# Cross-attention scores and weighted sums per head, in tiles of TensorE's array

## What is computed

```python
def _L0_xattn_ref(query, key, value, Wq, Wk, Wv, Wo, bo):
    DIM = 512
    NUM_HEADS = 16
    ...
    q = (query @ Wq).reshape(B, L, H, D).transpose(0, 2, 1, 3)
    k = (key @ Wk).reshape(B, S, H, D).transpose(0, 2, 1, 3)
    v = (value @ Wv).reshape(B, S, H, D).transpose(0, 2, 1, 3)
    attn = jnp.einsum('bhld,bhsd->bhls', q * SCALE, k)
    attn = jax.nn.softmax(attn, axis=-1)
    x = jnp.einsum('bhls,bhsd->bhld', attn, v)
    x = x.transpose(0, 2, 1, 3).reshape(B, L, C)
    return x @ Wo + bo
...
x = x + _L0_xattn_ref(_layernorm(x, axis=-1), ctx_1024, ctx_1024, ...)
x = x + _L0_attn_ref(_layernorm(x, axis=-1), ...)
x = x + _L0_ffn_ref(_layernorm(x, axis=-1), ...)
```

## Time and profile before

| what | value |
|---|---|
| median of three runs | 2842.11 us (2841.47 to 2845.34) |
| the profiled execution | 2842.77 us |
| its span in the trace | 2841.0 us |
| PE busy | 2720.9 us (96%), 17864 matmuls |
| DVE, ACT, POOL busy | 1657.8, 1246.9, 774.1 us |
| cross attention, by its first key matmul and the last adds of outputs | 142.89 to about 1933 us |

### The profile page before, as it was taken

One profiled execution on the slowest core, in us unless ns is written; L12 is line 12 of the kernel. 1 busy time (PEld: TensorE's weight loads), 2 busy tenths in 40 slices (PEclk: granted clock), 3 DMA queues, 4 the chain that ended last, 5 costly groups with the idle time before them and its releaser, 6 DMA issues. The chain is left out here.

```text
span 2841.0 us, 53482 instructions
## 1 busy us (share of the span) xinstructions
PE 2720.9 (96%) x17864; PEld 1635.0 (58%) x17864; DVE 1657.8 (58%) x3658; ACT 1246.9 (44%) x2898; POOL 774.1 (27%) x1530
## 2 busy tenths in 40 slices
PE   7999999999999999999999999995898998998999
PEld 4555555555555555555555555553466666666666
DVE  7645555555555555555555555556666666676675
ACT  4344444444444444444444444442444444444444
POOL 2133333333333333333333333321111111111110
PEclk9999999999999999999999999997899999999999
DMA  3311111111111111111111111103100000000000
GB/s 137 108 44 63 43 42 42 42 42 42 42 43 48 42 42 42 42 42 42 42 44 47 42 42 42 42 13 100 52 31 16 16 30 15 15 30 15 15 23 16
DMA packets 65959, 118.47 MB, mean 42 GB/s; under 512 B 12017, under 2 KB 32497, under 8 KB 65393
## 3 DMA queue, kind: packets, MB, share of 16 engines
q1 hardware_dynamic: 65904, 117.76, 12.7%
HBM read 109.06 MB, written 8.65 MB: 41 GB/s over the span
## 5 line engine op out<-in xcount | busy, mean ns | idle before, releaser
L746 DVE SCALAR_TENSOR_TENSOR kT_lo<-psum,kT_hi 128x512 f16<-128x512 f32 x256 | 177.0, 692 | 447.3 <-ACT kT_hi L677 447.3
L681 ACT ACTIVATE v_hi<-psum 128x512 f16<-128x512 f32 x256 | 153.1, 598 | 551.1 <-PE psum L836 551.1
L123 POOL TENSOR_TENSOR c_lo<-ctx_raw,c_hi 128x1024 f16<-128x1024 f32 x128 | 272.3, 2128 | 447.7 <-ACT c_hi L673 422.4
L836 PE MATMUL psum<-c_hi,xWk_hi 128*128 128x512 f16 x1024 | 388.1, 379 | 0.5 <-PEq L143 0.5
L836 PE MATMUL psum<-xWv_hi,c_hi 128*128 128x512 f16 x1024 | 388.1, 379 | 0.0
L836 PE MATMUL psum<-xWv_lo,c_hi 128*128 128x512 f16 x1024 | 388.1, 379 | 0.0
L836 PE MATMUL psum<-xWv_hi,c_lo 128*128 128x512 f16 x1024 | 388.1, 379 | 0.0
L836 PE MATMUL psum<-c_lo,xWk_hi 128*128 128x512 f16 x1024 | 388.1, 379 | 0.0
L836 PE MATMUL psum<-c_hi,xWk_lo 128*128 128x512 f16 x1024 | 388.1, 379 | 0.0
L752 DVE SCALAR_TENSOR_TENSOR v_lo<-psum,v_hi 128x512 f16<-128x512 f32 x256 | 177.1, 692 | 360.7 <-ACT v_hi L681 360.7
L687 ACT ACTIVATE e<-psum,neg_max 128x257 f32<-128x257 f32 x512 | 237.3, 476 | 281.7 <-DVE neg_max L741 281.7
(11 more groups left out here) (227 smaller groups left out, 5715.6 us busy)
## 6 DMA issues: line engine op xcount, KB each, us to landing
ctx_raw<-in_ctx_main SPq DMA_DIRECT2D x128, 512.0 KB, 3.3
xs<-in_x SPq DMA_DIRECT2D x8, 1024.0 KB, 5.4
v_rep<-v_last_rows SPq DMA_DIRECT2D x512, 16.0 KB, 2.3
xb<-in_x SPq DMA_DIRECT2D x16, 512.0 KB, 3.6
out<-res_out SPq DMA_DIRECT2D x32, 256.0 KB, 2.1
ffn_raw<-in_w_t SPq DMA_DIRECT2D x11, 512.0 KB, 3.8
res<-in_w_t SPq DMA_DIRECT2D x5, 512.0 KB, 4.0
xs<-in_late_w SPq DMA_DIRECT2D x2, 1024.0 KB, 4.8
```

The source lines that it names most:

```text
L123: nc.gpsimd.tensor_tensor(c_lo[u // 2][:, :, u % 2, :], c_raw[u % 2][:, :, :], c_hi[u // 2][:, :, u % 2, :], ALU.subtract).then_inc(c_lo_d ...
L681: nc.scalar.mul(v_hi[u][:, t, :], v_bank(t), W_UNSCALE).then_inc(v_hi_done, 1)
L746: nc.vector.scalar_tensor_tensor(out=kT_lo[r][:, m, :, 0:S], in0=k_bank(m), scalar=W_UNSCALE, in1=kT_hi[r][:, m, :, 0:S], op0=ALU.mult, op ...
L836: mm = nc.tensor.matmul(bank, a, b, start=(n == 0), stop=(n == len(steps) - 1))
```

## The change

Scores and outputs are made per head, on parts of PE's array. A matmul whose operands lie in a strip of 32 partitions, and whose result goes to a strip of 32 PSUM partitions, takes one 32 x 32 tile of the array; one with 128 operand partitions and 32 result partitions takes a column strip of 128 x 32.

- `score`: weights are the queries of one head, 32 x 32, taken from `q_hi` or `q_lo`, two buffers each; the head (g, h) sits in partition strip h and writes to partition strip g of bank h. There are 3 passes x 4 x 4 = 48 matmuls of 257 columns, the passes outermost. No zeros are multiplied.
- `outputs`: for each h, six steps of four matmuls, one for each strip g: weights are 128 context tokens by the 32 latent rows of a head, 32 columns of values are streamed. There are 4 x 6 x 4 = 96 matmuls into bank 3, partition strip g, columns 32 h to 32 h + 31.
- The roles of g and h are swapped in PSUM and behind it: `gather_output` is one 128 x 128 add where there were four of 32 x 128; the value rows of the last token are kept in natural order; Wo's rows are permuted on loading, by four DMAs (`load_output_weight`) instead of one.
- POOL: `stage_queries` makes two copies of 128 x 128 where `spread` made eight of 32 x 128, and may run one element further ahead, since there are two buffers; the two memsets go.
- PE's five waits before the scores are put before the last matmul of the `values` ahead of them (`score_may_start`).

```diff
-                nc.scalar.mul(vl[:, :].rearrange("p (h g d) -> p g h d", h=4, g=KC),
-                              v_last_bank.rearrange("p (g h d) -> p g h d", h=4, g=KC),
-                              W_UNSCALE).then_inc(vl_done, 1)
+                nc.scalar.mul(vl[:, :], v_last_bank, W_UNSCALE).then_inc(vl_done, 1)
...
-        bd_hi = sb_in(ctx, "bd_hi", [P, KC, HPG, L], F16)
-        bd_lo = sb_in(ctx, "bd_lo", [P, KC, HPG, L], F16)
+        q_hi = [sb_in(ctx, f"q_hi{u}", [P, KC, L], F16) for u in range(2)]
+        q_lo = [sb_in(ctx, f"q_lo{u}", [P, KC, L], F16) for u in range(2)]
...
-        out_bank = psum[:, 3, :].rearrange("p (g n) -> p g n", g=KC)
+        out_bank = psum[:, 3, 0:P].rearrange("p (h d) -> p h d", h=HPG)
...
+            def load_output_weight():
+
+                rows = late_w[0].rearrange("(i d) (g n) -> g d i n", i=HPG, g=KC)
+                to = late_raw.rearrange("p o (c n) -> p (o c) n", c=KC)
+                for g in range(KC):
+                    sp.dma_start(to[32 * g:32 * g + 32, :, :], rows[g]).then_inc(late_landed, 16)
...
-            def spread(b, contexts):
-
-                past(pool, s_ps, b)
+            def stage_queries(b, u, contexts):
+
+                past(pool, s_ps, b - 1)
...
-                for h in range(HPG):
-                    rows = slice(32 * h, 32 * h + 32)
-                    nc.gpsimd.tensor_copy(bd_hi[rows, :, h, :],
-                                          heads_hi[rows, :, bass.ds(b * L, L)]).then_inc(bd_ready, 1)
-                    nc.gpsimd.tensor_copy(bd_lo[rows, :, h, :],
-                                          heads_lo[rows, :, bass.ds(b * L, L)]).then_inc(bd_ready, 1)
+                for heads, q in ((heads_hi, q_hi), (heads_lo, q_lo)):
+                    nc.gpsimd.tensor_copy(q[u % 2][:, :, :], heads[:, :, bass.ds(b * L, L)]
+                                          ).then_inc(q_ready, 1)
...
-                for h in range(HPG):
-                    rows = slice(32 * h, 32 * h + 32)
-                    nc.vector.tensor_tensor(o_sum[rows, :, :], out_bank[rows, :, 32 * h:32 * h + 32],
-                                            last_part[rows, :, :], ALU.add).then_inc(o_sum_done, 1)
+                nc.vector.tensor_tensor(o_sum[:, :, :], out_bank, last_part[:, :, :], ALU.add
+                                        ).then_inc(o_sum_done, 1)
...
+                for n, (a, b) in enumerate(steps):
+                    if score_next and n == len(steps) - 1:
+                        score_may_start(*score_next)
+                    mm = nc.tensor.matmul(v_bank(t), a, b, start=(n == 0), stop=(n == len(steps) - 1))
+                mm.then_inc(v_ps, 1)
...
-                for g in range(KC):
-                    mm = run(psum[:, g, 0:S + 1],
-                             [(q[:, g, :, :].rearrange("p h l -> p (h l)"), k[u // 2][:, g, u % 2, 0:S + 1])
-                              for q, k in passes(bd_hi, bd_lo, kT_hi, kT_lo)])
+                past(pe, o_sum_done, b)
+
+            def score(i, u):
+                steps = passes(q_hi[u % 2], q_lo[u % 2], kT_hi, kT_lo)
+                for n, (q, k) in enumerate(steps):
+                    for g in range(KC):
+                        for h in range(HPG):
+                            rows = slice(32 * h, 32 * h + 32)
+                            mm = nc.tensor.matmul(psum[32 * g:32 * g + 32, h, 0:S + 1], q[rows, g, :],
+                                                  k[u // 2][rows, g, u % 2, 0:S + 1], start=(n == 0),
+                                                  stop=(n == len(steps) - 1))
...
-                for g in range(KC):
-                    cols = slice(g * P, (g + 1) * P)
-                    mm = run(out_bank[:, g, :], [(p[:, t, cols], v[:, t, cols]) for t in range(ST)
-                                                 for p, v in passes(pT_hi, pT_lo, v_hi[u % 2], v_lo[u % 2])])
+                for h in range(HPG):
+                    steps = [(p[:, t], v[:, t]) for t in range(ST)
+                             for p, v in passes(pT_hi, pT_lo, v_hi[u % 2], v_lo[u % 2])]
+                    for n, (p, v) in enumerate(steps):
+                        for g in range(KC):
+                            mm = nc.tensor.matmul(out_bank[32 * g:32 * g + 32, h, :],
+                                                  p[:, h * P + g * 32:h * P + g * 32 + 32],
+                                                  v[:, g * P + h * 32:g * P + h * 32 + 32], start=(n == 0),
+                                                  stop=(n == len(steps) - 1))
```

More of the change, by code:

```diff
@@ L553, in cross_attention @@
         late_lo_done = sem_in(ctx, "late_lo_done")
-        names = ["bd_clear", "bd_ready", "k_col", "last_done", "k_ps", "v_ps",
+        names = ["q_ready", "k_col", "last_done", "k_ps", "v_ps",
                  "s_ps", "p_ps", "pv_ps", "k_hi_done", "k_lo_done", "v_hi_done", "v_lo_done", "max_done",
@@ L557, in cross_attention @@
                  "o_norm_done", "o_T_done", "o_hi_done", "o_lo_done"]
-        (bd_clear, bd_ready, k_col, last_done, k_ps, v_ps, s_ps, p_ps, pv_ps,
+        (q_ready, k_col, last_done, k_ps, v_ps, s_ps, p_ps, pv_ps,
          k_hi_done, k_lo_done, v_hi_done, v_lo_done, max_done, neg_done, e_done, pT_hi_done, pT_lo_done,
@@ L603, in _ @@
                 load_last(b, b)
-            with sp.Fori(0, LATE) as i:
+            load_output_weight()
+            quad(0)
+            with sp.Fori(1, LATE) as i:
                 quad(i, late=True)
@@ L639, in last_token @@
                 b = i * 4 + u
-                pool.wait_ge(bd_ready, 2 * HPG * (b + 2 if more else b + 1))
+                pool.wait_ge(q_ready, 2 * (b + 2 if more else b + 1))
                 pool.wait_ge(e_done, KC * (b + 1))
                 pool.wait_ge(rep_landed[u % 2], 16 * HPG * (i * 2 + u // 2 + 1))
-                past(pool, o_sum_done, HPG * b)
+                past(pool, o_sum_done, b)
                 nc.gpsimd.tensor_tensor(last_part[:, :, :], v_rep[u % 2][:, :, :],
@@ L651, in step @@
                 if more:
-                    spread(b + 1, b + 4 if ahead else BATCH)
+                    stage_queries(b + 1, u + 1, b + 4 if ahead else BATCH)
                 last_token(i, u, more)
@@ L657, in step @@
                     low_context(nc, pool, contexts, b + 4, u)
-            spread(0, 0)
-            pool.wait_ge(bd_ready, 2 * HPG)
+            stage_queries(0, 0, 0)
+            pool.wait_ge(q_ready, 2)
             last_keys(0, 0)
@@ L699, in high_late @@
             def high_late(n, c):
-                act.wait_ge(late_landed, 16 * (n + 1))
+                act.wait_ge(late_landed, 16 * (n + KC))
                 nc.scalar.mul(late_hi_w[:, bass.ds(n * 2, 1), c * D:(c + 1) * D],
@@ L769, in gather_output @@
                 dve.wait_ge(last_done, b + 1)
[L770 to L773 removed]
+                nc.vector.tensor_tensor(o_sum[:, :, :], out_bank, last_part[:, :, :], ALU.add
+                                        ).then_inc(o_sum_done, 1)
             def finish_output(b):
[L776 removed]
+                dve.wait_ge(o_sum_done, b + 1)
                 dve.wait_ge(inv_done, b + 1)
@@ L844, in keys, with values, score_may_start @@
                                 for w, c in passes(wk_hi, wk_lo, c_hi[r], c_lo[r])]).then_inc(k_ps, 1)
-            def values(b, u, t):
+            def values(b, u, t, score_next=None):
                 past(pe, v_lo_done, ST * (b - 1) + t + 1)
                 rows = slice(t * P, (t + 1) * P)
-                run(v_bank(t), [(c[:, k, u % 2, rows], w[:, k, :]) for k in range(KC)
-                                for c, w in passes(c_hi[u // 2], c_lo[u // 2], wv_hi, wv_lo)]
-                    ).then_inc(v_ps, 1)
-            def score(i, u):
+                steps = [(c[:, k, u % 2, rows], w[:, k, :]) for k in range(KC)
+                         for c, w in passes(c_hi[u // 2], c_lo[u // 2], wv_hi, wv_lo)]
+                for n, (a, b) in enumerate(steps):
[3 more added lines that the diff above has]
+                mm.then_inc(v_ps, 1)
+            def score_may_start(i, u):
                 b = i * 4 + u
-                pe.wait_ge(bd_ready, 2 * HPG * (b + 1))
+                pe.wait_ge(q_ready, 2 * (b + 1))
                 pe.wait_ge(k_col, 2 * (i * 2 + u // 2 + 1))
@@ L895, in step @@
                 if more:
-                    values(b + 1, (u + 1) % 4, 1)
+                    values(b + 1, (u + 1) % 4, 1, score_next=(i, u + 1) if u < 3 else (i + 1, 0))
             for m in range(KC):
@@ L900, in _ @@
             values(0, 0, 0)
-            values(0, 0, 1)
+            values(0, 0, 1, score_next=(0, 0))
             with pe.Fori(0, QUADS - 1) as i:
```

5 lines of the change are left out of this document (removed).

## The result

| kernel | median of runs, us | ratio to before (95%) |
|---|---|---|
| before | 2842.22 (2841.47 to 2845.34) | |
| with the change | 2933.12 (2915.61 to 2941.26) | 1.0311 (1.0271 to 1.035) |

The change made the kernel 91 us slower, where 82 us faster was forecast. The profiled execution took 2939.93 us with a span of 2938.0.

A forecast was written before the change was run, and what follows sets the result against it. PE was taken to bound cross attention; per element -1.29 us from tiles and +0.65 from switches gave -0.64, times 128 = -82 us, so 2760 us. Its own range was 2640 to 2820, the 8-in-10 range 2640 to 3060.

The forecast's parts named there:

- What bounds the kernel: Cross attention: PE busy without a hole, 13.88 us per element; savings in scores and outputs count 128 times.
- The pace: Tiled scores and outputs: 9.5 ns from pair to pair, 1.37 us instead of 2.66, so -1.29 us per element.
- The switches: Into and out of tiled scores and outputs: four layout changes of 0.163 us, +0.65 us per element.
- Moved waits: Score waits placed 0.216 us earlier, ahead of the last values matmul: cost nothing, with 0.9 us of slack for o_sum.
- the way to the end: From scores to transposes and outputs: slack of 1.48 and 0.74 us holds, so PE's gain reaches the end.
- the other engines: POOL's copies about -1.5 us on an engine idling 66%; SP's four weight DMAs cost nothing; token stages unchanged.
- The rival of the longer loop: PE's loop of 800 pairs is fetched again, 2.3 us in each of 31 rounds: +71, 2832 us; chance 0.05.
- The rival of pairs one at a time: Tiled scores and outputs: every pair takes 25.3 ns whatever its place, 2967 to 3051 us; chance 0.30.
- What would show it: Signs in PE's timeline: score and output times, switch holes, period 13.24 us, transposes and outputs not waiting, granted clock 1.00.

The follow-up runs named there:

- e1: The changed kernel with TensorE's cross-attention loop written out for all 31 rounds: 2719.45 us, ratio 0.9571.
- e5: The changed kernel with its loop turned, beginning at the transposes and ending with the next element's keys: 2718.45 us, ratio 0.9561.
- e9: The changed kernel with 72 extra one-column matmuls (144 instructions) ahead of its untouched loop: 2724.08 us, ratio 0.9581.
- e12: The kernel before with the outputs alone as 96 products of 128x32 strips: 2792.61 us, ratio 0.9825.
- e16: The changed kernel with its loop written out and the five waits put back right before the scores: 2718.86 us, ratio 0.9566.
- e17: The changed kernel with its loop turned and a body of eight elements (1600 pairs, 15 rounds): 2724.62 us, ratio 0.9583.
- e8: The kernel before with TensorE's loop body written out for eight elements (736 pairs): 2841.24 us, ratio 0.9997.
- e4: The changed kernel with an unturned loop body of eight elements (1600 pairs, 15 rounds): 2846.97 us, ratio 1.0018.
- e6: The changed kernel, loop written out, with the outputs' strip loop outermost so that pairs of one strip follow each other: 2776.55 us, ratio 0.9764.
- e7: The kernel before with TensorE's cross-attention loop written out for all 31 rounds: 2843.19 us, ratio 1.0.
- e3: The kernel before, without tiles, with a loop body of twelve elements (1104 pairs): 2854.07 us, ratio 1.0043.
- e18: The changed kernel with its four-element loop turned and 91 extra one-column matmuls (182 instructions) ahead: 2767.19 us, ratio 0.9732.
- e10: The changed kernel with 128 extra one-column matmuls (256 instructions, one packet) ahead of its loop: 2927.26 us, ratio 1.0274.
- e13: The changed kernel with 36 extra one-column matmuls (72 instructions) ahead of its loop: 2977.25 us, ratio 1.0471.

## Why the prediction was wrong

- *What bounds the kernel*: right. PE was busy all the time, and all that the tiles saved came out at the end as soon as the loop didn't stall (e1, e5, e9).
- *The pace*: 9.5 ns was taken, between 6.3 and 12.6. Measured: scores 0.64 us, outputs 0.86, together 1.50, of which some 0.2 are the switches out of them, so 1.3 against the forecast's 1.37. The 23 groups of four strips from 1004.86 to 1005.58 make 0.72 us / 92 pairs = 7.8 ns a pair.
- *The switches*: a term that was over-sized, at 0.163 us each, bounded by 0 and 0.26. From the last 512-column matmul to the first tiled one it is 1008.41 - 1008.10 = 0.31 us instead of 0.216, so 0.09 on the way in; on the way out the last four outputs start from 1005.58 on, over some 0.03 us, and `values` begin at 1005.72, about 0.1. Four come to some 0.4 us, not 0.65. With it the element is at -0.94 us instead of -0.64. "TensorEngine Tiling (Array Packing)" of the Trainium skill, Key Properties, says that a change of mode drains TensorE; a wait of 0.1 us is there, shorter than the 0.163 us of pipe that I equated with a drain. The same page's ban on the fast weight load for column tiling (Feature Incompatibilities) did not undo the outputs' gain: e12 gains 50 us. Whether it costs something is not shown.
- *Moved waits, the way to the end, the other engines*: right outside the jumps. The maxima start 1.64 us after the last `values` matmul has had its 0.216 us (1009.96 - 1008.32), as before (1.63), and one 128 x 128 add takes 0.28 us. e16 shows the waits to be free in straight code; their share at a stalled jump, about 0.4 us by the rows above, is not tested.
- *The rival of the longer loop*: this is the step that failed. The sum took the loop of 800 pairs to be held like the one of 668 and put its jumps at nothing. The rival that priced them had the mechanism right, as e1, e9 and e17 show; its chance (0.05) and its price (2.3 us in each of 31 rounds, which would still have been faster than before) were not. Two things were mis-sized. First the room: I took the loop to fit because 668 pairs do, and leaned on "Runtime: NRT & Kernel Launch" of the Trainium skill, Instruction fetch mechanics, with its 2048 instructions for TensorE. The loop has 1632 to 1645, and is held or not by its place, seven packets against eight; held were also 736 pairs (e8). The same section says that a taken branch to a page that isn't there stalls for its fetch, and the traces agree, with 3.59 us in the row above and 3.3 to 6.7 us in the jumps' own records; it has the crossing of a block as mostly hidden, which e1 confirms for straight code, with no stall in 228 packets. Second the price: there were two holes a round, 6.4 us, one at the jump and one at the end of the first packet, which 47 tiled pairs reach before the next one has come (in e4 as few as 5), and the clock fell to its lower level behind them: 9.3 us a stalled round, 24 of them, 223 us. The forecast of -82 became -123 by the tiles, less 223 lost at jumps: 2715.4 + 223 = the span of 2938.
- *The rival of pairs one at a time*, which held 0.30, is ruled out: even the same strip again goes at 13.6 ns, below the 14 from which it would decide. The range of 2640 to 3060 held the result by luck, thanks to a rival that wasn't its cause.
- *What would show it*: this part named the right rows (transposes, granted clock), and the clock of 0.95 was the first sign; waits of PE for issue and the count of instruction packets should have been among them.

## What to carry to other kernels

When an edit multiplies the instructions of a hardware loop on TensorE, count them in packets of 256 and compare with the largest loop that is known to be held (here one that touches seven packets). Near that size the time depends on where the loop begins, and a change elsewhere in the program can gain or lose 7 to 9%. Put the jump back behind the longest matmuls of the body. What counts is the work that is still queued when the jump is issued, so avoid semaphore waits right ahead of it; this last advice is argued from the rows, not tested. The turned body of eight elements gained 122 us (e17 against e4); the other way is to write the loop out. Look at instruction packets and at waits for "issue" before judging a change of the arithmetic: here it was a gain of 4.3% that read as a loss of 3.1%.

## What the runs showed of the hardware

- With the switch behind them, 48 pairs of 32 x 32 weights and 257 columns take 0.64 us, 13 ns a pair; 96 pairs of 128 x 32 weights and 32 columns 0.86 us with different strips in turn and 1.31 us (0.86 + 0.45) with the same strip six times in a row.
- A switch between the whole array and tiles, or back, costs about 0.1 us (1008.41 - 1008.10 - 0.216, and the outputs' end at 1005.6 to 1005.72).
- A straight stream of instructions was fetched without any stall (e1, e6, e7, e16). A jump back to held instructions took 0.21 us of the sequencer, one that fetches 3.3 to 3.9 us (e3, e17, e18) or 4.5 to 6.7 (the changed kernel, e4, e10, e13). PE stood still for what the queued matmuls left of it: 4 us with 1.5 us queued, 1.3 with 2.8 (1.1 in the view of waits), about 0.1 with 3.7. A second wait, mostly of 1 to 3 us, came at the end of the first packet where that was 5 to 47 pairs behind the jump.
- A loop of about 1640 instructions was held where it touched seven packets of 256, fetched whole (nine packets a jump) where it touched eight, and went both ways at the edge. Shorter loops (783 and 1564 records of PE a round, before and e8) were held and longer ones (2345, e3; 3286, e4) fetched, at the one place tried for each. That seven is the limit for loops of another make is not shown, and so stays open why at the edge 24 of 30 jumps stall.
